# The cross-attention sum moved from a matmul to VectorE, the row maxima split over three engines, and new call lists, in a decoder layer on one core

## The reference

```python
x = x + attn(layernorm(x), Wq, Wk, Wv, Wo)      # 16 heads of 16, scores * tril, then softmax
x = x + xattn(ctx, ctx, layernorm(x), ssm_kernel, D)   # kv = outer product per head of 8, long convolution
                                                # with ssm_kernel along the tokens, + kv * D, then times q
x = x + ffn(layernorm(x), gate/up/down in 4-bit codes with scales)   # 256 -> 2048 -> 256
```

## Time and profile before

| | |
|---|---|
| median of 3 runs | 259.4 us |
| the profiled execution | 259.37 us, of which the span from the first to the last instruction is 257.7 us |
| PE busy | 243.9 us (95%) |
| DVE, ACT, POOL busy | 158.0, 128.6, 146.1 us |
| mean granted TensorE clock | 0.993 |

### The profile page before, as it was taken

The page is one execution under the profiler, slowest core; times in us unless marked ns, Lnnn a source line. Parts: engine busy times, 40 slices in busy tenths (PEclk is TensorE's granted clock), DMA queues, the critical chain, the costliest instruction groups (busy, mean ns, idle before and its releaser), DMA issues.

```text
span 257.7 us, 5017 instructions
## 1 busy us (share of the span) xinstructions
PE 243.9 (95%) x1872; PEld 158.6 (62%) x1872; DVE 158.0 (61%) x271; ACT 128.6 (50%) x281; POOL 146.1 (57%) x189
## 2 busy tenths in 40 slices
PE   7999999999989999796999999999999999999993
PEld 7755776556666666474545677566566566565562
DVE  1887687778889899898369775327145182322124
ACT  2354666467688678554766353315333343523230
POOL 4267455841649699989599941283453635433230
PEclk9999999999999999979999999999999999999999
DMA  6996996903340004000120000003030000000004
GB/s 174 378 341 191 164 258 183 163 13 115 126 126 1 4 3 127 3 0 0 51 75 0 3 0 0 3 1 122 3 94 28 3 1 0 3 0 0 0 3 163
DMA packets 15104, 18.81 MB, mean 73 GB/s; under 512 B 1448, under 2 KB 12776, under 8 KB 15080
## 3 DMA queue, kind: packets, MB, share of 16 engines
q1 hardware_dynamic: 15080, 18.49, 26.3%
HBM read 15.21 MB, written 3.15 MB: 71 GB/s over the span
## 4 chain that ended last, share of the span: by engine, by line
PE 75%; POOL 12%; DVE 5%; issue 3%; ACT 2%; DMA 2%; SPq 0%; DVEq 0%; POOLq 0%; ACTq 0%
PE bank L1242 38%; PE bank L1408 16%; POOL arena L447 4%; PE bank L1296 4%; PE bank L1298 3%; PE bank L1300 3%; POOL arena L450 2%; POOL rstd L358 2%; DMA X<-in_x 2%; PE bank L1314 2%; PE bank L1482 2%; POOL shift L360 1%; PE bank L1480 1%; DVE XN L1208 1%; POOL w L463 1%
## 5 line engine op out<-in xcount | busy, mean ns | idle before, releaser
L1033 DVE SCALAR_TENSOR_TENSOR QK<-bank,QK 128x512 f32<-128x512 f32 x32 | 22.1, 690 | 64.0 <-PE bank L1242 61.9
L471 POOL TENSOR_TENSOR QK<-QK 128x512 f16<-128x512 f32 x24 | 27.8, 1159 | 56.6 <-ACT QK L643 56.6
L653 ACT ACTIVATE QK<-bank 128x512 f32<-128x512 f32 x32 | 19.1, 597 | 65.2 <-PE bank L1242 65.2
L1242 PE MATMUL bank<-xTh,Wa 128*128 128x512 f16 x128 | 40.5, 379 | 0.2 <-DVE xTl L1056 0.2
L1242 PE MATMUL bank<-xTh,Wb 128*128 128x512 f16 x128 | 40.7, 379 | 0.0
L447 POOL TENSOR_TENSOR arena<-Ys,qx 128x640 f32<-128x640 f32 x16 | 25.7, 1606 | 4.6 <-ACT qx L705 4.6
L1242 PE MATMUL bank<-xTl,Wa 128*128 128x512 f16 x64 | 24.3, 379 | 0.0
L1242 PE MATMUL bank<-xTl,Wb 128*128 128x512 f16 x64 | 24.3, 379 | 0.0
L967 DVE TENSOR_REDUCE mx<-bank 128x8 f32<-128x1024 f32 x16 | 19.5, 1219 | 6.7 <-PE bank L1331 6.7
L1408 PE MATMUL bank<-Wa,QK 128*128 128x256 f16 x192 | 23.4, 273 | 0.0
L1408 PE MATMUL bank<-Wb,QK 128*128 128x256 f16 x192 | 23.3, 273 | 0.0
(11 more groups left out here) (148 smaller groups left out, 497.9 us busy)
## 6 DMA issues: line engine op xcount, KB each, us to landing
arena<-in_codes SPq DMA_DIRECT2D x6, 384.0 KB
arena<-in_ker SPq DMA_DIRECT2D x2, 1024.0 KB, 12.6
QK<-qk_scratch SPq DMA_DIRECT2D x8, 256.0 KB, 5.6
arena<-in_ctx SPq DMA_DIRECT2D x2, 768.0 KB, 8.8
qk_scratch<-Wa SPq DMA_DIRECT2D x12, 128.0 KB, 3.4
arena<-in_gu_scale SPq DMA_DIRECT2D x6, 256.0 KB
QK<-qk_scratch SPq DMA_DIRECT2D x8, 128.0 KB, 5.5
out<-XN SPq DMA_DIRECT2D x4, 256.0 KB, 2.4
```

What stands on the lines that cost most here:

```text
L471: g_.tensor_tensor(il[:, u % IR], val[:, u % VR], ih[:, u % IR], ALU.subtract).then_inc(s_il, 1)
L653: s_.activation(val[:, u % VR], bank[2 * (u % 2)][:, :], ACT.Gelu_apprx_tanh, scale=1.0 / W_GAIN).then_inc(s_gel, 1)
L1033: v_.scalar_tensor_tensor(out=val[:, u % VR], in0=bank[2 * (u % 2) + 1][:, :], scalar=UP_SCALE, in1=val[:, u % VR], op0=ALU.mult, op1=ALU. ...
L1242: ins = mmul(out, a(c), w(c), start=(n == 0), stop=(n == 3 * len(chunks) - 1))
```

## The change

Four things change.

1. `add_cross(b)` no longer multiplies X by the identity on PE. It only transposes the two halves of R into bank 6; `stats_ffn(b)` on DVE then adds the bank to X, and `take_cross(b)` on ACT goes. `project_out(b)` keeps its X times identity.
2. The pieces of the maxima: DVE makes `ms` (behind the second `pair_max` of a sequence), ACT makes the high part (`max_hi`, with `exp_max` behind it), POOL only the low part.
3. `take_query(b)` is one eviction that writes each head's eight numbers twice, in place of two that wrote them once and in rotated order; `conv_products` reads it at other offsets.
4. The call lists of all four engines are new.

```diff
@@ max_pieces (POOL)
-                pool.wait_ge(s_max, 2 * b + 2)
-                if b >= 2:
-                    pool.wait_ge(s_em, b - 1)
-                    pool.wait_ge(s_mpt, b - 1)
+                pool.wait_ge(s_mhi, b + 1)
...
-                g_.tensor_scalar(ms[:, r], mx[:, r], guard[:, 0:1], 1.0 / MAX_GAIN, ALU.max, ALU.mult).then_inc(s_ms, 1)
-                g_.tensor_scalar(hi, view(mx[:, r], by_half), guard[:, 0:1], 1.0 / MAX_GAIN,
-                                 ALU.max, ALU.mult).then_inc(s_ms, 1)
-                pool.wait_ge(s_ms, 2 * b + 2)
                 g_.tensor_tensor(lo, view(ms[:, r], by_half), hi, ALU.subtract).then_inc(s_mch, 1)
@@ new on ACT
+            def max_hi(b):
+
+                sc.wait_ge(s_ms, b + 1)
+                if b >= 2:
+                    sc.wait_ge(s_mpt, b - 1)
+                s_.activation(view(mp[:, b % 2], [[16, 2], [4, 2], [1, 4]]),
+                              view(ms[:, b % 2], [[4, 2], [8, 2], [1, 4]]), ACT.Copy).then_inc(s_mhi, 1)
+                exp_max(b)
@@ take_cross (ACT) goes, take_query (ACT) is one instruction
-            def take_cross(b):
-
-                sc.wait_ge(s_rt, b + 1)
-                s_.activation(X[:, b, :], bank[6][:, 0:D], ACT.Copy).then_inc(s_x2, 1)
...
-                s_.activation(view(qx[:, b % 2], [[16, 2 * H], [1, HD]], 4),
-                              view(bank[6][:, :], [[HD, 2 * H], [1, HD]]),
-                              ACT.Copy).then_inc(s_qx, 1)
-                s_.activation(view(qx[:, b % 2], [[16, 2 * H], [12, 2], [1, 4]]),
-                              view(bank[6][:, :], [[HD, 2 * H], [-4, 2], [1, 4]], 4),
+                s_.activation(view(qx[:, b % 2], [[16, 2 * H], [HD, 2], [1, HD]]),
+                              view(bank[6][:, :], [[HD, 2 * H], [0, 2], [1, HD]]),
                               ACT.Copy).then_inc(s_qx, 1)
@@ pair_max (DVE)
+                if p == 1:
+                    ve.wait_ge(s_max, n + 1)
+                    if b == 0:
+                        ve.wait_ge(s_const, 7)
+                    if b >= 2:
+                        ve.wait_ge(s_em, b - 1)
+                    v_.tensor_scalar(ms[:, b % 2], mx[:, b % 2], guard[:, 0:1], 1.0 / MAX_GAIN,
+                                     ALU.max, ALU.mult).then_inc(s_ms, 1)
@@ stats_ffn (DVE)
             def stats_ffn(b):
 
+                ve.wait_ge(s_rt, b + 1)
+                v_.tensor_tensor(X[:, b, :], X[:, b, :], bank[6][:, 0:D], ALU.add).then_inc(s_x2, 1)
                 ve.wait_ge(s_x2, b + 1)
                 ln_stats(2, b)
@@ add_cross (PE)
                 pe.wait_ge(s_r, 2 * b + 2)
-                pe.wait_ge(s_x1, b + 1)
-                mmul(bank[6][:, 0:D], ident[:, :], X[:, b, :], start=True, stop=False, skip_group_check=True)
                 for c in range(2):
-                    last = mmul(bank[6][:, P * c:P * c + P],
-                                R[:, b % 2, H * c:H * c + H, :].rearrange("p h i -> p (h i)"),
-                                ident[:, :], start=False, stop=(c == 1), skip_group_check=True)
+                    last = t_.transpose(bank[6][:, P * c:P * c + P],
+                                        R[:, b % 2, H * c:H * c + H, :].rearrange("p h i -> p (h i)"), ident[:, :])
                 last.then_inc(s_rt, 1)
```

More of the change, by code:

```diff
@@ L734, in _ @@
             conv_out(7, 0)
+            max_hi(0)
             conv_out(7, 1)
@@ L766, in _ @@
             take_out(0)
+            pv_out(1)
+            probs(2, 0)
+            ln_eps(1, 0)
+            max_hi(4)
             probs(2, 1)
-            ln_eps(1, 0)
+            ln_apply(1, 0)
+            take_heads(1)
+            take_query(0)
+            pv_out(2)
+            take_out(1)
             probs(3, 0)
-            pv_out(1)
+            take_max(4)
+            ln_eps(1, 1)
             probs(3, 1)
-            ln_apply(1, 0)
-            pv_out(2)
+            ln_apply(1, 1)
@@ L785, in _ @@
-            probs(5, 0)
-            ln_apply(1, 1)
-            take_query(1)
-            take_out(2)
-            pv_out(4)
-            take_heads(3)
+            take_heads(3)
+            probs(5, 0)
+            ln_apply(1, 2)
+            pv_out(4)
+            ln_eps(2, 0)
+            take_out(3)
+            take_query(2)
+            take_max(6)
+            max_hi(7)
             probs(5, 1)
-            ln_eps(1, 2)
-            take_cross(0)
-            take_out(3)
+            ln_apply(2, 0)
@@ L1082, in _ @@
             skip_tap(5)
-            products(4)
+            products(0)
             skip_tap(6)
+            q_lo(0, 3)
             skip_tap(7)
+            q_lo(1, 0)
+            q_lo(1, 1)
+            products(1)
+            q_lo(1, 2)
+            q_lo(1, 3)
             skip_tap(8)
@@ L1126, in _ @@
             pair_max(6, 1)
-            normalise(2)
-            sum_slots(0, 0)
-            stats_cross(1)
+            stats_cross(2)
+            sum_slots(0, 1)
+            normalise(3)
+            stats_ffn(0)
             pair_max(7, 0)
-            normalise(3)
-            sum_slots(0, 1)
+            sum_slots(1, 0)
             pair_max(7, 1)
-            stats_cross(2)
-            decode_codes(3)
+            sum_slots(1, 1)
             stats_cross(3)
-            sum_slots(1, 0)
@@ L1560, in _ @@
             attend(2, 1)
+            turn_heads(1)
+            attend(2, 2)
+            turn_query(0)
+            attend(2, 3)
+            project_out(1)
             key_scores(3, 0)
-            attend(2, 2)
-            attend(2, 3)
+            turn_values(2)
+            attend(3, 0)
+            turn_max(4)
             key_scores(3, 1)
             row_scores(6, 0)
-            turn_values(1)
-            key_scores(4, 0)
-            turn_max(5)
-            turn_query(0)
-            row_scores(6, 1)
-            attend(3, 0)
             attend(3, 1)
```

442 lines of the change are left out of this document (214 added, 228 removed).

## The result

The changed kernel takes **257.78 us** (median of 7 executions, 256.15 to 258.57). The kernel before, run on the same chip, takes 259.58 us (259.3 to 259.95). The ratio is 0.9917, with a 95% interval of 0.9895 to 0.9938. The ratio leaves out every execution that took over 1.5% more than the fastest of its kernel. The forecast of 257.3 us was 0.5 us too low, and its sign and its range held. The two terms of its sum did not fit the profiled execution: one missed by -0.7 us and the other by +1.7 us. That errors of opposite sign nearly cancel is luck.

What follows compares the result with a forecast made beforehand. PE's own work was taken to bound the feed-forward, and PE and DVE by turns the stretch before it. -0.75 us before gate_and_up(0) and -1.3 us after it gave -2.05 us on 259.37: 257.3 us, range 253.6 to 261.0 us.

Steps and rivals of the forecast that it cites:

- whatever PE work goes there is gained in full, if nothing new makes it wait: From 124 to 155 us PE is busy for 30.97 of 31 us, so PE work saved there counts in full.
- The feed-forward stretch: From gate_and_up(0) to the end: PE's add_cross and turn_query work goes from 3.99 to 2.70 us, -1.3 us.
- two transposes of the same size, for which I keep 0.45 us: In add_cross, the two transposes were priced like the two products with R they replace, 0.45 us.
- The stretch up to gate_and_up(0): Ahead of the feed-forward: PE's count -2.15 us, DVE's +1.3 us, middle -0.45, with ln_apply(2, 3)'s 0.3 us: -0.75 us.
- I take the middle: Up to gate_and_up(0), both engines bound by turns, so -0.45 us between PE's -2.15 and DVE's +1.3 us.
- The prediction's own sign of it: Second term wrong if PE's gaps before the feed-forward grow by more than 2 us, waiting for `o_sb` or the sums R.
- The wait at convolve(9, 1): A sign against the second term: convolve(9, 1), right behind turn_max(0) in bank 7, must let ACT read first; no size.
- counted only as what keeps DVE's sums from waiting: POOL loses 6.5 us of max_pieces instructions, 3.3 us behind 74 us; that alone moves nothing on PE.
- ln_apply(2, 3) moved: On ACT, ln_apply(2, 3) goes ahead of take_out(7), so turn_ffn(3) may follow at once: up to 0.7 us, taken as 0.3.
- The rival of the clock: A second clock fall, at the attention's end, costs 1.6 us: 258.9 us; chance 0.20 with every other way within 0.3%.
- The slower rival: DVE, with decode_codes(3) directly ahead of ffn_lo(3), sets the start of the feed-forward: +2.5 us, 261.9 us; chance 0.18.
- The greater gain: Sequences run closer: PE's 2.15 us in full and POOL's 2.58 us wait for qx(1) gone: -6.05 us, 253.3 us; chance 0.20.

Runs made afterwards that it cites:

- Runs 1: The kernel before, old call lists, with only the cross-attention's addition to X moved to DVE and the sums of R transposed: 262.09 us, ratio 1.0105.
- run 4: The kernel before, old call lists, with all three edits (addition on DVE, maxima's pieces on three engines, one query eviction): 262.05 us, ratio 1.0091.
- run 5: The changed kernel with add_cross turning the sums by plain products with the identity in place of transposes: 258.82 us, ratio 0.9955.
- run 2: The kernel before, old call lists, with only the maxima's pieces split over DVE, ACT and POOL: 259.60 us, ratio 1.0003.
- Run 6: The changed kernel with ffn_lo(2) ahead of o_sb of sequence 7 on DVE: 256.24 us, ratio 0.9871.
- run 10: The kernel with ffn_lo(2) ahead of o_sb, and on ACT take_out(6) ahead of ln_eps(2, 3), take_heads(7) ahead of ln_eps(1, 5): 255.73 us, ratio 0.9858.
- run 7: The changed kernel, new lists kept, with all the maxima's pieces made by POOL again: 265.81 us, ratio 1.0230.
- run 11: The changed kernel with `ms` on DVE but both pieces made by POOL and no Copy on ACT: 258.78 us, ratio 0.9959.

## Why the prediction was right, and where it was wrong

*What bounds the kernel.* Right: PE's own work behind gate_and_up(0), and waits of all engines by turns ahead of it. What I did not see is how close the full stretch was to its next bound. I read 30.97 of 31 us as "whatever PE work goes there is gained in full, if nothing new makes it wait", and walked only through the new lists. Runs 1 and 4 show that on the old lists the same saving ends in waits, in more and deeper falls of the clock, and 2.3 us slower by the median.

*The feed-forward stretch, forecast -1.3 us, measured -2.0.* The mechanism was right and one price was wrong: "two transposes of the same size, for which I keep 0.45 us", and the same for turn_query. A pair takes 0.22 us (run 5 has both forms side by side, and its stretch is 2.16 us longer than the changed kernel's: 4 x 0.23 for the four plain add_cross and 1.25 for gate_and_up(0) at the low clock). With it the sum is 3 x 0.88 + 3 x 0.22 = 3.30 us before and 6 x 0.22 = 1.32 us after, -2.0 us, which is the measured stretch. The row was to be had: turn_query lies in the chain of before between 126.78 and 127.00 us, and I took add_cross's products with R in its place.

*The stretch up to gate_and_up(0), forecast -0.75 us, measured +0.97.* "I take the middle" between PE's count and DVE's was no argument, and this is the step that failed, by 1.7 us. The prediction's own sign of it came: PE's gaps ahead of the feed-forward grew by more than 2 us (9.33 to 11.37). They did not come "behind a DVE without gaps", though. DVE has 5.9 us idle in the 26 us, more than before. The additions cost 409 ns on the mean, as priced. `ms` costs 417 ns on the mean, not 250: seven of the eight take 0.23 to 0.47 us and one takes 1.27 us. Against that o_sb takes 600 ns on the mean where it took 1,068. That POOL has less to do is not the reason: in run 2 POOL is relieved of the same 16 instructions on the old lists and o_sb takes 1,077 ns. It is the order of calls, by which fewer o_sb meet a long instruction of POOL (last section). The wait at convolve(9, 1), which I had named, came too, and is 0.4 us.

What set the start is an interplay of order and clock. ffn_lo(2) queues behind o_sb of sequence 7, PE waits 2.14 us, the clock falls, and the chain from there to gate_and_up(0) goes through project_out(6) and (7) with nothing beside them to hide the lower clock. With the clock kept the kernel takes 256.6 us, against 259.4 to 259.6 before; with the -2.0 us of the stretch, the start would then be 0.8 to 1.0 us earlier than before (an estimate; no trace of the changed kernel has the clock kept). So the forecast's 0.75 us fits where the clock was kept, and of the miss of 1.7 us in the profiled execution about 1.5 are the fall of the clock at its new place, which I had as a rival and at nothing in the sum. Run 6 moves one call and has the start at 124.18 us; run 10 moves two more and has it at 123.02, 1.0 us ahead of before and within 0.3 us of the forecast's 123.28 (124.03 - 0.75).

*POOL, "counted only as what keeps DVE's sums from waiting".* Half right. On the old lists the edit is worth nothing (run 2). With the new lists it is what they stand on: 8.0 us in run 7. And at least 7.0 of these are not POOL's busy time, but that exp_max on ACT asks POOL's queue for `ms` (run 11).

*ln_apply(2, 3) moved, -0.3 us.* Not seen by itself. turn_ffn(3) follows take_out(7) at once in the chain after, as I said it might.

*The rival of the clock.* It came true in four of seven executions. In the profiled one the clock falls from 116 to 120 us, behind two us in which PE is busy for 0.67 of 2. In executions with a mean clock of 0.993 the changed kernel takes 258.1 us (mean of 4), and with the clock kept 256.6 (mean of 3): 1.5 us, which is my price of 1.6 us, taken from the earlier trace rows. In the kernel before the same fall costs almost nothing: 259.8 us (34 executions from 0.985 to 0.994) against 259.6 us (23 with the clock kept). Run 2, whose list behind 100 us is that of before, shows what covers it there, for its profiled execution had the clock at 1.00 all through. The kernel before takes 2.57 us for project_out(5) at the low clock, run 2 takes 1.3 at the high one. But PE then waits for ffn_lo(2), which stands behind o_sb of sequence 7, and in both DVE works without a gap from 109 us to the end of that o_sb, at about 118. The first row is of before with the fall, the second of run 2 without it (turn_heads(7) in both):

```profile
118.84 0.44 PE L1445 MATMUL bank<-ident,o_sb 128*128 128x128 f32 x2 [0.93 <-DVE xTl L1056]
```

```profile
118.97 0.44 PE L1462 MATMUL bank<-ident,o_sb 128*128 128x128 f32 x2 [1.46 <-DVE xTl L1073]
```

PE, 1.3 us faster, waits that much longer (1.46 us here and 0.7 in three short waits ahead, against 0.93), and turn_heads(7) starts at the same time. In the changed kernel the fall comes behind the wait for ffn_lo(2), where nothing is left to cover it. The gap alone does not decide whether the clock falls: ahead of the place PE is busy for 0.96 of 2 us in run 2, without a fall, and for 0.95 before, with one. The Trainium skill, TensorE: Matmul & The Clock Gate, section Part 4: PE-mode transpose, says that transposes in that mode do not count as PE being busy in the same way. Run 5 does not bear out that it matters here: with plain products the clock falls in half of the executions too. A shorter gap does go with a kept clock: run 6 took away 1.2 us of waiting, and none of its 6 executions fell below a mean of 0.996.

*The slower rival*, decode_codes(3) ahead of ffn_lo(3), was wrong: DVE still stands idle for 1.68 us between the decoding and ffn_lo(3), for which it waits for ACT. *The greater gain*, 253.3 us, did not come. The part of it that run 10 finds (255.7 us) lies in the tail of the attention, not in POOL's wait for the query of sequence 1.

## What to carry to other kernels

When an engine is full for a long stretch, look for what is nearly late beside it (here the queries of the upper sequences, which come by way of POOL's queue), before counting that engine's saved work as gain. An edit and its call lists are one change: by the medians the edits alone cost 2.3 us, the lists gave 4.3, and one instruction left on the wrong queue cost 7. Where two engines bound a stretch by turns, follow the chain call by call through the new order to its end rather than taking a middle: three calls moved by one or two places were worth 2 us. And compare executions of like clock before putting a difference down to the order of calls: of these 2 us about half is that the clock no longer falls.

## What the hardware showed that was not expected

- Two fp32 transposes of 128 columns take 0.22 to 0.24 us where two plain fp32 products of the same size take 0.45 us (run 5 and the changed kernel, one trace each). The Trainium skill, TensorE: Matmul & The Clock Gate, section Terms, calls the mode four times faster for FP32; here it is twice. Behind a wait the same pair takes 0.4 to 0.5 us (0.48 in run 4).
- The same small instruction of DVE on 16 columns takes 0.23 us in some places and 1.27 us in another, while an instruction of POOL ran (timelines of the changed kernel's DVE, then POOL):

```profile
69.78 0.23 DVE L969 TENSOR_SCALAR ms<-mx,guard 128x16 f32<-128x16 f32 x1
...
85.67 1.27 DVE L969 TENSOR_SCALAR ms<-mx,guard 128x16 f32<-128x16 f32 x1
```

```profile
85.33 1.58 POOL L456 TENSOR_TENSOR w<-arena 128x768 f32<-128x768 fp8e4 x1
```

  It ends at 86.94 us, 0.03 us behind POOL's instruction. o_sb does the same: the six long ones of the kernel before (0.94 to 1.81 us) each begin while an instruction of POOL runs and end 0.27 to 0.28 us behind it, and the one of 1.69 us in the changed kernel ends 0.29 us behind POOL's. So the duration of such an instruction is set by when it starts, here the rest of POOL's instruction and a little. The other two of before take 0.42 us, and one of them starts 0.03 us behind an instruction of POOL, so that not every such meeting costs DVE.

- The same fall of the clock, of about 4 us, costs 0.2 us in one order of the calls and 1.5 us in another. A deeper one, to a mean clock of 0.976 to 0.980, came in 5 of 72 executions of the kernel before and cost it 3.7 us; it came in 5 of 9 of run 4. No trace of the kernel before has it.
